# A value product moved behind the next unit's first scores, and q/k stacks filled in halves

## The reference

```
h = relu(layernorm(x))
q, k, v = h @ Wq + bq, h @ Wk + bk, h @ Wv + bv          # (b, n, 8 heads, 32)
scores = q k^T / sqrt(32) + (1 - adj) * -1e9
out = softmax(scores) v                                  # back to (b, n, 256)
x = x + out @ Wo + bo
```

## Time and profile before

| | us |
|---|---|
| median of 3 runs | 1272.16 (1271.64 to 1273.63) |
| the profiled execution | 1269.52, of which its span is 1267.7 |
| TensorE matmul busy | 1170.4 (92%) |
| ScalarE busy | 993.3 (78%) |
| VectorE busy | 987.3 (78%) |
| GpSimd busy | 131.6 (10%) |
| mean granted TensorE clock | 0.991 of full speed |

### The profile page before, as it was taken

How to read it: one execution, slowest core, us unless ns; L and a number is a source line. 1 busy time by engine, 2 the same in 40 slices (tenths; PEclk the granted TensorE clock), 3 DMA queues, 4 the chain that set the end, 5 groups by cost and what they waited for, 6 DMA issues and landing times.

```text
span 1267.7 us, 30114 instructions
## 1 busy us (share of the span) xinstructions
PE 1170.4 (92%) x10752; PEld 885.5 (70%) x10752; DVE 987.3 (78%) x1802; ACT 993.3 (78%) x1827; POOL 131.6 (10%) x235
## 2 busy tenths in 40 slices
PE   4799999999989999899999999999998999999897
PEld 4576776777767776676766777767776767777665
DVE  4697786977878877887878877888777978778775
ACT  2588886887878977788877878778877888778885
POOL 4002000020001101021010210002000020000001
PEclk9799999999999999999999999999999999999999
DMA  8442061511505134051431515225061320615001
GB/s 278 112 94 75 18 151 36 120 49 40 140 25 134 35 68 117 19 134 35 96 89 27 127 35 127 61 56 124 5 150 53 71 64 1 163 39 113 22 2 51
DMA packets 53470, 100.06 MB, mean 79 GB/s; under 512 B 10032, under 2 KB 35888, under 8 KB 53296
## 3 DMA queue, kind: packets, MB, share of 16 engines
q1 hardware_dynamic: 52720, 96.25, 30.3%
q0 software_dynamic: 576, 1.57, 0.5%
HBM read 22.28 MB, written 8.39 MB: 24 GB/s over the span
## 4 chain that ended last, share of the span: by engine, by line
PE 62%; ACT 21%; issue 8%; DVE 6%; SPq 1%; DMA 1%; ACTq 0%; POOL 0%; DVEq 0%; POOLq 0%
PE ps_turn L681 18%; PE ps_heads L737 18%; PE ps_scores L667 12%; ACT rows L420 11%; ACT turned_p L427 6%; PE ps_side L688 4%; PE ps_side L697 4%; PE ps_side L716 4%; DVE turned_p L515 3%; ACT turned_p L433 2%; SPq L248 1%; DVE rows L504 1%; ACT ht L445 1%; PE ps_turn L688 1%; DVE stats L539 1%
## 5 line engine op out<-in xcount | busy, mean ns | idle before, releaser
L504 DVE CUSTOM_DVE_ANT_0 rows<-ps_scores,mask 128x1024 f32<-128x1024 f32 x512 | 623.2, 1218 | 49.8 <-issue 29.8
L420 ACT ACTIVATE rows<-rows,row_min 128x1024 f32<-128x1024 f32 x512 | 591.5, 1155 | 31.3 <-DVE row_min L504 16.0
L681 PE MATMUL ps_turn<-ident_r,rows_raw 128*128 128x128 f32 x4096 | 499.6, 258 | 53.4 <-DVE turned_p L515 23.9
L681 PEld LDWEIGHTS ps_turn<-ident_r,rows_raw 128*128 128x128 f32 x4096 | 407.7, 141 | 189.2 <-issue 88.2
L427 ACT ACTIVATE turned_p<-ps_turn 128x512 f32<-128x512 f32 x512 | 307.5, 601 | 193.3 <-PE ps_turn L681 191.8
L515 DVE COPY turned_p<-ps_turn 128x512 f32<-128x512 f32 x384 | 263.3, 686 | 173.4 <-PE ps_turn L681 171.6
L667 PE MATMUL ps_scores<-k_stack,q_stack 128*128 128x512 f32 x1024 | 360.9, 434 | 12.3 <-DMA k_stack<-k_lo 12.3
L737 PE MATMUL ps_heads<-turned_p,v 128*32 128x256 f32 x4096 | 247.4, 382 | 11.3 <-ACT turned_p L427 10.8
L737 PEld LDWEIGHTS ps_heads<-turned_p,v 128*32 128x32 f32 x4096 | 120.1, 109 | 107.4 <-ACT turned_p L427 33.7
L667 PEld LDWEIGHTS ps_scores<-k_stack,q_stack 128*128 128x128 f32 x1024 | 153.9, 190 | 14.6 <-issue 7.7
L397 POOL COPY inv_wide<-row_inv 128x256 f32<-128x256 f32 x64 | 25.5, 398 | 1054.1 <-DVE row_inv L551 956.4
(11 more groups left out here) (55 smaller groups left out, 463.3 us busy)
## 6 DMA issues: line engine op xcount, KB each, us to landing
k_stack<-k_hi SPq DMA_DIRECT2D x128, 128.0 KB, 2.4
k_stack<-k_lo SPq DMA_DIRECT2D x128, 128.0 KB, 2.4
q_stack<-q_lo SPq DMA_DIRECT2D x124, 128.0 KB, 2.4
q_stack<-q_hi SPq DMA_DIRECT2D x120, 128.0 KB, 2.4
res<-in_x SPq DMA_DIRECT2D x32, 256.0 KB, 2.7
out<-res SPq DMA_DIRECT2D x32, 256.0 KB, 2.2
xn<-in_x SPq DMA_DIRECT2D x7, 1024.0 KB, 6.1
mask<-in_adj SPq DMA_DIRECT2D x1, 3584.0 KB, 14.8
```

The lines of the kernel that those rows point to most:

```text
L420: nc.scalar.activation(rows[:, m % RING, :], rows[:, m % RING, :], ACT.Exp, bias=row_min[:, m % RING:m % RING + 1], scale=-1.0, accum_out= ...
L504: nc.vector.tensor_tensor_reduce(out=rows[:, m % RING, :], in0=ps_scores[m % 2][:], in1=mask[:, qt, :], scale=1.0, scalar=START_MIN, op0=A ...
L681: tr = nc.tensor.transpose(bank[:, k, :].bitcast(F32R), rows_raw[:, i % RING, kt * P:(kt + 1) * P], ident_r[:])
```

## The change

- **Value product.** `heads` of a unit stands whole in slot 0 of the next unit, behind both halves of `turn` and the scores of row 4. The turned rows have a new layout (`turned`, nine places, two of them for row 0 in turn), since row 0 of the next unit is now turned and copied before the product has read the old one.
- **Inverse sums.** `invert` and `turn_inv` stand in slot 7 of the unit itself (`INV_ROW` = 7), `turn_inv` behind the side work. `copy_inv` stands in ScalarE's slot 0, `heads` waits for it (both use one PSUM bank), and `norm_heads` stands in slot 4.
- **ScalarE's order.** `high_part`, `copy_ht` and `copy_inv` stand ahead of the slot's `exp`; before, they stood behind it.
- **Moments.** One tile in each of slots 10 to 17 of phase 0, behind `copy_b`.
- **Stacks.** `hi` and `lo` hold 512 tokens instead of 1024. After each `qk` step SyncE issues 16 DMAs of 64 KB, so 64 for a phase. `high_part` of step 2 waits until those of steps 0 and 1 have landed.
- **Side table.** The same steps in other slots. The value bias is folded into the output bias (`bo_row`) at the start. `HEAD` = 10. In the diff the first `slot` is ScalarE's, the second TensorE's.

```
-    (("qk", 0, (1, 1, 2, 2)), ("o", 3, (3, 3, 4, 4)), ("qk", 1, (5, 5, 7, 7)), ("qk", 2, (9, 9, 11, 11)),
-     ("qk", 3, (13, 13, 14, 14)), ("v", 0, (17, 18, 19, 19)), ("v", 1, (21, 21, 22, 22)),
-     ("ht", 0, (26, 26, 26, 26)), ("ht", 1, (27, 27, 27, 27)), ("ht", 2, (29, 29, 29, 29)),
-     ("ht", 3, (30, 30, 30, 30))),
-    (("v", 0, (1, 1, 3, 3)), ("qk", 0, (5, 5, 6, 6)), ("qk", 1, (8, 8, 8, 8)), ("qk", 2, (10, 10, 11, 11)),
-     ("qk", 3, (13, 13, 14, 14)), ("v", 1, (16, 16, 17, 17)), ("o", 0, (18, 18, 20, 20)),
-     ("o", 1, (22, 22, 25, 25)), ("o", 2, (27, 29, 29, 29))),
+    (("qk", 0, (1, 1, 2, 2)), ("o", 3, (5, 6, 7, 7)), ("qk", 1, (9, 9, 10, 10)), ("qk", 2, (12, 13, 14, 15)),
+     ("qk", 3, (17, 17, 18, 18)), ("v", 0, (20, 20, 21, 21)), ("v", 1, (23, 23, 25, 25)),
+     ("ht", 0, (27, 27, 27, 27)), ("ht", 1, (28, 28, 28, 28)), ("ht", 2, (29, 29, 29, 29)),
+     ("ht", 3, (30, 30, 30, 30))),
+    (("qk", 0, (1, 1, 2, 2)), ("v", 0, (4, 4, 5, 5)), ("qk", 1, (6, 6, 7, 7)), ("v", 1, (9, 9, 10, 10)),
+     ("o", 0, (13, 14, 15, 15)), ("qk", 2, (17, 17, 18, 18)), ("qk", 3, (20, 21, 22, 22)),
+     ("o", 1, (25, 25, 26, 26)), ("o", 2, (29, 29, 30, 30))),
...
+STATS = {HEAD + t: t for t in range(TILES)}
...
             def slot(b, g, i, first, last):
+                kind, s, pieces = side_work(g, i - 1, first, last)
+                if kind == "ht" and done:
+                    copy_ht(b + 1, s)
+                if kind == "qk" and done:
+                    for h in range(PARTS):
+                        if s == 0:
+                            act.wait_ge(stacked[g][h], stack_count(g, b + 1))
+                        elif s == 2:
+                            act.wait_ge(stacked[ng][h], stack_count(ng, nb, 2))
+                    high_part(nb, ng, s, hi[s % 2][:])
+                if r == 0 and not (first and i == 0):
+                    copy_inv(unit(b, g, i // UNIT_ROWS) - 1)
                 m = ahead(g, i, EXP_AHEAD)
                 if not (last and m >= BATCH_ROWS):
                     exp(m, row(b, 0, m))
                 copy_a(b, g, i)
...
             def slot(b, g, i, first, last):
-                for half in range(2):
-                    if i % UNIT_ROWS == 0 and not (first and i == 0):
-                        heads(n, unit(b, g, u), g if u else 1 - g, half)
-                    turn(b, g, i, half)
+                turn(b, g, i, 0)
+                turn(b, g, i, 1)
                 m = ahead(g, i, SCORES_AHEAD)
                 if not (last and m >= BATCH_ROWS):
                     scores(m, row(b, 0, m), True, fills)
+                if r == 0 and not (first and i < UNIT_ROWS):
+                    for half in range(2):
+                        heads(unit(b, g, u) - 1, u + 1, g if u else 1 - g, half)
...
+                if r == INV_ROW:
+                    turn_inv(b, g, u, first)
```

More of the change, by code:

```diff
@@ L262, in load_res, with wait @@
                              ).then_inc(res_in[u % 2], 16)
[L264 to L271, removed]
+            def wait(done, count):
+                count = held(sp, count)
+                sp.wait_ge(lo_done, QK_STEPS)
+                sp.wait_ge(done, count)
@@ new lines, in _, with spread, unit_work @@
+                stack_start(pool, start_stacked[h], h, "q", range(POOL_COPIES))
+            pool.wait_ge(bo_ready, 1)
+            def spread(b, g, u):
+                count = held(pool, unit(b, g, u) + 1)
+                own()
+                pool.wait_ge(inv_done, count)
+                pool.wait_ge(inv_turned, count)
+                pool.tensor_copy(inv_wide[:], row_inv[:].unsqueeze(2).to_broadcast([P, UNIT_ROWS, HEAD_DIM])
+                                 ).then_inc(inv_spread, 1)
+            def unit_work(b, g, u, last):
+                spread(b, g, u)
+                if (g, u) == (0, 0):
+                    add_bias(b, 0)
+                elif (g, u) == (0, 1) and not last:
+                    norm(b + 1)
+                elif (g, u) == (0, 2):
+                    add_bias(b, 1)
+                elif (g, u) == (1, 2):
+                    add_bias(b, 2)
+                elif (g, u) == (1, 3):
+                    add_bias(b, 3)
@@ L471, in slot @@
                     exp(m, row(b, 0, m))
[L473 to L484 removed]
                 copy_a(b, g, i)
[L486 removed]
+                if r in ACT_COPIES:
                     copy_b(b, g, i)
[L489 to L492 removed]
+            slots(act, slot)
+            copy_inv(BATCH * BATCH_UNITS - 1)
         @block.vector
@@ L602, in slot @@
-                if kind == "o" and done:
-                    finish(b * UNITS + (0 if g == 0 else s + 1), s)
-                if g == 0 and not last:
-                    for t in STATS.get(i, ()):
-                        moments(b + 1, t)
-                u = i // UNIT_ROWS
-                if not (first and i < HEAD):
-                    pg, pu = (g, u - 1) if u else (1 - g, UNITS - 1)
-                    if i % UNIT_ROWS == 0:
-                        invert(unit(b, g, u), pu)
-                    if i % UNIT_ROWS == NORM_ROW:
-                        norm_heads(unit(b, g, u), pg, pu)
@@ L615, in slot @@
-                if i % UNIT_ROWS not in ACT_COPIES:
+                    mask_row(m, row(b, 0, m), m % ROWS // PARTS)
+                kind, s, pieces = side_work(g, i - 1, first, last)
+                if PIECES - 1 in pieces:
+                    nb, ng = next_phase(b, g)
+                    if kind == "qk":
+                        low_part(nb, ng, s, lo[s % 2][:], hi[s % 2][:])
+                    elif kind == "v":
+                        copy_v(nb, ng, s)
+                    elif kind == "o":
+                        finish(b * UNITS + (0 if g == 0 else s + 1), s)
@@ L616, in slot @@
+                if r == INV_ROW:
+                    invert(b, g, u, first)
+                if r not in ACT_COPIES:
                     copy_b(b, g, i)
+                if r == NORM_ROW and not first:
+                    norm_heads(unit(b, g, u) - 1, *((g, u - 1) if u else (1 - g, UNITS - 1)))
+                if g == 0 and i in STATS and not last:
+                    moments(b + 1, STATS[i])
             def tail():
-                units = BATCH * BATCH_UNITS
-                invert(units, UNITS - 1)
@@ L644, in side_wait @@
                     return
-                kind, s, _ = side_work(pg, pi, first, last)
-                nb, ng = (b, 1) if pg == 0 else (b + 1, 0)
+                back, kind, s = before
+                pb_, pg = (b, g) if not back else (b, 0) if g == 1 else (b - 1, 1)
+                nb, ng = next_phase(pb_, pg)
                 if kind == "qk":
```

381 lines of the change are left out of this document (194 added, 187 removed).

## The result

The changed kernel takes 1338.53 us (1337.69 to 1341.82), the kernel before 1272.89 us in the same comparison; the ratio is 1.052, 95% interval 1.049 to 1.054. It is slower, as forecast, but by 65.6 us where 43 were forecast, and 3.5 us above the end of the range.

The account below looks back on a forecast made before the run. TensorE bounds the mean, but three engines run at almost the same pace after a value product. A batch gains 5.9 us: 41 over seven batches, 3 more in the last, so 1313.5, forecast 1315 (1290 to 1325; full range 1256 to 1335).

Parts of the forecast that it names:

- The queue behind it pays on: After TensorE's 1.44 us wait for a copy queued behind high_part, two more waits of about 0.4 us follow.
- ScalarE's order: Exponential queued behind high_part and copy_ht: 0.5 to 0.9 us each time not hidden, 4 to 6 us a batch.
- the walk: Units followed instruction by instruction, using distances between starts in the timelines: 156.9 us for all eight units.
- One sign: In the profile after, TensorE's waits for VectorE's copies should be about as long as before or longer.
- Inverse sums: turn_inv waits in TensorE's queue where VectorE inverts late: together about 3.7 us a batch.
- the length of unit 1 of phase 0: VectorE's copies, masks and statistics before the inversion make this the longest unit, 21.0 us.
- The sum: Eight units, 0.8 us for stacks and 2.0 for the restart: a batch takes 159.7 us against 153.8.
- Moments: VectorE's statistics in slots 10 to 15 of phase 0: five tiles of 0.60 us, 3.0 us before the inversion.
- Restart: The loop's restart, after what ScalarE and VectorE regain in it: 2.0 us a batch.
- Stacks: SyncE's 64 KB DMAs: value product waits 1 to 2 us by count, nothing by bytes; taken 0.8 us a batch.
- The rival "faster": Helpers are further ahead than walked, so the savings stand alone: together 30 us, 1242 us; chance 0.21.
- TensorE's saving from an undivided product: Value product in one piece saves 0.2 to 0.3 us a unit, 13 to 19 us over 64 units.

Follow-up runs that it names:

- e4_before_late_exp: The kernel before, with only ScalarE's exponential moved behind copy_inv, copy_ht and high_part: 1320.71 us, ratio 1.038.
- e1_exp_first: The kernel after, with ScalarE's exponential back at the front of its slot: 1308.67 us, ratio 1.029.
- e3_invert_first: The kernel after, with invert put ahead of the mask of VectorE's slot 7: 1342.18 us.
- e2_no_moments: The kernel after, with the statistics of batches 1 to 7 left out (batch 0's used instead): 1341.15 us.
- e5_qk1_early: The kernel after, with phase 0's output step in slots 5, 5, 6, 6 and qk step 1 in 7, 7, 8, 8: 1331.88 us, ratio 1.049.
- e6_qk1_early_no_moments: e5_qk1_early with the statistics of batches 1 to 7 left out as well: 1313.80 us, ratio 1.034.
- e13_after_unrolled: The kernel after with its loops written out, the instructions otherwise the same: 1331.17 us, ratio 1.047.
- e9_loop_at_unit: e5_qk1_early with exponential and invert first in their slots, statistics in slots 12, 15 and 16, loop boundary at slot 8 instead of 10: 1295.99 us, ratio 1.019.
- e11_copy_inv_first: e9_loop_at_unit with copy_inv at the front of ScalarE's slot 0: 1284.13 us.

## Why the prediction was right and wrong

**Direction and mechanism: right.** "The queue behind it pays on" held: ScalarE's order was a large part (50 us in e4_before_late_exp, 30 us in e1_exp_first, 28 to 42 forecast), and the stall behind a high part was 1.31 us where the walk had 1.44. The unit lengths of phase 1 and of units 0 and 3 came out within 0.2 us, and unit 1 of phase 0 was the longest. One sign did not come: TensorE's waits for VectorE's copies fell from 23.9 to 15.2 us instead of staying.

**Inverse sums: the size right, the worth not.** 24.7 us of waits were found where 3.7 us a batch were forecast. Taking them away alone gave nothing (e3_invert_first).

**The step that failed is the length of unit 1 of phase 0.** The sum gave it 21.0 us and 2.0 for the restart. It had 25.8 on average in the six middle batches, 2.8 more, in two of them without any fall of the clock before its end. Two terms of VectorE's chain, which the walk had rightly made the limit, were too small:

- *Moments.* The walk took 0.60 us a tile, the distance between two neighbours in a run of four. A tile that stands alone between a copy and a mask costs 0.76 to 0.81 (395.69 to 396.45), since the mask starts only behind the aggregate. The five tiles before the inversion cost 3.9 us where 3.0 were forecast. The statistics stand beside SyncE's chain of about the same length, so leaving them out gave 0 in e2_no_moments, and 18 us only when the DMAs were early (e5_qk1_early to e6_qk1_early_no_moments).
- *Restart.* It was taken at 2.0 us, a number for which no row was shown. TensorE's own idle time at it is only 0.8 to 1.2 us, which looks like an error to the good side. But VectorE idles 2.7 to 3.3 us there, where it idles 0.17 in the first batch that has no restart, and VectorE sets the pace: 2.8 us a restart. Without restarts unit 1 was 3.0 us shorter (e13_after_unrolled).

The rest is the product's wait for `copy_inv`, which the sum had under the stacks, and 0.3 us at the unit's end.

**The clock: no term at all.** The sum took every duration from rows at the full clock, and the waits that it forecast were themselves what the clock fell behind, for 3 to 14 us in each batch. In unit 1 the fall cost next to nothing, since TensorE is not the limit there. Where it reached the value product and the slots behind it, it cost 1.3 to 1.8 us: unit 2 of phase 0 takes 19.75 us without a fall and 21.1 to 21.5 with one, in five of the eight batches. With two lesser cases that is 8 to 9 us over the run. That TensorE is 88% busy over the span does not tell it; windows of a few microseconds do.

**Stacks: right in seven batches, partly by luck.** The prediction stood between two bounds, an issue by bytes (0.30 us) and by count (0.59 us), and took 0.8 us a batch between them. Count was right (0.59 us for either size), and the row for it was there. That should have made 1 to 2 us, but the product waited only 5.2 us in the first seven batches together: VectorE's chain behind the first of these DMAs was longer than forecast and hid the rest. In the last batch, which has no statistics, it waited 3.64 us where the sum had nothing. The page of the Trainium skill that was named, "DMA: Bandwidth & Descriptors", section Bandwidth, says that transfers under 64 KB are bound by their descriptors. These have just 64 KB, and the trace agrees in direction: 0.59 us of issue at 64 KB and at 128 KB, landing in 2.0 and 2.4 us. With the count, step 1's DMAs reach just past the end of unit 1, and whatever shortens that unit meets them.

These four together, about 6 us for the moments, 5 for the restarts, 8 to 9 for the clock and 3.6 for the last batch, make some 23 us of the 23.5 by which the median missed. They are read from one trace by adding up units; no run takes each out alone. A start some 2 us later and small differences of both signs about cancel.

**The rival "faster"** had its price right in one way: TensorE's saving from an undivided product shows (the two halves' records start 1.75 us apart, before 1.86 plus the switch). With all repairs and no restarts the new order is as fast as the old one (1249.84 and 1249.89 us). No run moved the value product alone, so its own worth is not shown; what the runs show is that all parts together bring nothing once they are ordered well, and that ScalarE's order, the statistics and `copy_inv` decided the loss.

**What stays open:** which waits exactly set off the lower clock (unit 0 of the kernel after has a stall of 1.31 us without a fall), and why TensorE's idle time at the restart is short behind a value product.

## What to carry to other kernels

In an in-order queue, put work that waits for another engine's last result behind the work whose input is already there: here ScalarE stood idle 1.14 us for a projection while an exponential whose row was ready queued behind, and swapping the two cost 30 to 50 us over 512 rows. Price an instruction by its distance in the surrounding in which it will stand: the statistics' 0.60 us held only in a run of four. Ask of a pause, such as a loop's restart, what it costs the engine that sets the pace, not the one that is busiest. When two chains end together, take both away before you call either free. Where a forecast contains new idle time of TensorE, give it a term for the granted clock, and read that in windows of some microseconds, not over the span.

## What the runs showed of the hardware

- The issue of a DMA from SyncE took 0.59 us for 32 rows of 4 KB and for 32 rows of 2 KB alike; only the landing changed, 2.4 to 2.0 us.
- A loop's restart left TensorE idle 2.2 to 2.7 us ahead of slot 7 (kernel before), 3.0 to 4.6 ahead of slot 8 (e9_loop_at_unit to e11_copy_inv_first) and 0.8 to 1.2 ahead of slot 10 (kernel after). ScalarE and VectorE idled too, VectorE 2.7 to 3.3 us in the kernel after. Written out, the 30,000 instructions of the kernel before ran 22 us faster, and TensorE's matmuls show no wait for "issue".
- A tile's statistics cost VectorE 0.60 us in a run of four tiles and 0.76 to 0.81 us alone between a copy and a mask.
- The granted clock fell to the 1.2 GHz level for some 3 or 7 us at a time behind stretches in which TensorE was busy 5.4 of 8 us or 2.6 of 5 us. A single stall of 1.31 us between busy stretches left it at 2.4 GHz in unit 0 of the looped kernel, while without the loop the clock fell in that unit behind one of 1.39 us.
- What a fall costs depends on who sets the pace: half a value product took 3.45 us instead of 1.93 and its unit 1.5 us more, while unit 1, paced by VectorE, had 25.6 us with and without it.
